# Four layers in one kernel: the ranking's place at the start, the clip's place in the adapter stage, and three smaller moves

## The reference

```python
# layers 1 and 3
q, k, v = x @ Wq, x @ Wk, x @ Wv
attn = softmax(q k^T * 512**-0.5)                       # within a batch, 64 x 64
attn_out = (attn @ v) @ Wp + bp
cms_out = gelu(attn_out @ cW1 + cb1) @ cW2 + cb2 + one_hot(target_codes, 512)
modifier = gelu(concat([attn_out, cms_out]) @ mW1 + mb1) @ mW2 + mb2
x = clip(x + cms_out + modifier, 0.0, 1.0)
# layers 2 and 4
h = gelu(x @ W_down[role] + b_down[role])               # 512 -> 256
y = x + h @ W_up[role] + b_up[role]                     # 256 -> 512
x = (y - mean(y)) * rsqrt(var(y) + 1e-5) * gamma[role] + beta[role]
```

## Time and profile before

| | |
|---|---|
| timed runs | 2047.40, 2045.91, 2047.27 us; median 2047.27 |
| the profiled execution | 2048.77 us, span 2046.9 us, mean granted clock 0.997 |
| TensorE | 2026.1 us busy (99%), 9500 matmuls |
| VectorE | 1513.8 us busy (74%), 2353 instructions |
| ScalarE | 1019.4 us busy (50%) |
| GpSimd | 360.6 us busy (18%) |
| DMA | 169.77 MB, mean 83 GB/s |
| chain that ended last | TensorE 94%, VectorE 4%, ScalarE 1%, issue 1% |

### The profile page before, as it was taken

How to read it: one execution, slowest core, us unless ns; L and a number is a source line. 1 busy time by engine, 2 the same in 40 slices (tenths; PEclk the granted TensorE clock), 3 DMA queues, 4 the chain that set the end, 5 groups by cost and what they waited for, 6 DMA issues and landing times.

```text
span 2046.9 us, 27676 instructions
## 1 busy us (share of the span) xinstructions
PE 2026.1 (99%) x9500; PEld 1692.3 (83%) x9500; DVE 1513.8 (74%) x2353; ACT 1019.4 (50%) x1844; POOL 360.6 (18%) x382
## 2 busy tenths in 40 slices
PE   8999999999999999999999999999999999999998
PEld 7888888888888888888888888888888888888887
DVE  6576677887757667888877666888886766778877
ACT  5464544555355454555436454555544544445552
POOL 0011103222101102233000111233200111032221
PEclk9999999999999999999999999999999999999999
DMA  7401111213321112112460111112243011211142
GB/s 283 172 22 52 52 67 62 72 43 129 145 83 31 63 52 73 38 71 73 145 242 21 52 62 67 37 73 73 72 183 107 11 62 43 77 62 52 57 145 94
DMA packets 42376, 169.77 MB, mean 83 GB/s; under 512 B 5624, under 2 KB 9720, under 8 KB 34808
## 3 DMA queue, kind: packets, MB, share of 16 engines
q1 hardware_dynamic: 42096, 167.97, 23.6%
q10 hardware_dynamic: 144, 0.03, 0.0%
HBM read 146.97 MB, written 21.01 MB: 82 GB/s over the span
## 4 chain that ended last, share of the span: by engine, by line
PE 94%; DVE 4%; ACT 1%; issue 1%; DMA 0%; SPq 0%; DVEq 0%; ACTq 0%
PE psum L667 88%; PE psum L961 1%; PE psum L998 1%; PE psum L742 1%; PE psum L764 1%; DVE acc L1694 0%; ACT xz L1375 0%; DVE fpart L1425 0%; DVE yt L1897 0%; DVE yt L1901 0%; DVE stats L1880 0%; DMA fraw<-fuse_in 0%; PE psum L765 0%; PE psum L744 0%; SPq L421 0%
## 5 line engine op out<-in xcount | busy, mean ns | idle before, releaser
L667 PE MATMUL psum<-hs,wd 128*128 128x512 f32 x1920 | 448.8, 389 | 0.5
L667 PEld LDWEIGHTS psum<-hs,wd 128*128 128x128 f32 x1920 | 360.0, 188 | 76.9 <-DVE acc L1694 2.2
L667 PE MATMUL psum<-cop,wsm 128*128 128x512 f32 x1416 | 354.7, 389 | 0.0
L667 PE MATMUL psum<-aop,wsm 128*128 128x512 f32 x1320 | 333.0, 389 | 0.0
L667 PEld LDWEIGHTS psum<-cop,wsm 128*128 128x128 f32 x1416 | 265.8, 188 | 55.2
L667 PE MATMUL psum<-aop,wsc 128*128 128x512 f32 x1320 | 311.3, 389 | 0.0
L667 PEld LDWEIGHTS psum<-aop,wsm 128*128 128x128 f32 x1320 | 247.7, 188 | 51.5
L667 PEld LDWEIGHTS psum<-aop,wsc 128*128 128x128 f32 x1320 | 247.4, 188 | 51.4
L1670 DVE TENSOR_TENSOR acc<-psum,acc 128x1024 f32<-128x1024 f32 x144 | 175.7, 1220 | 87.4 <-PE psum L667 87.3
L1694 DVE TENSOR_TENSOR acc<-psum,acc 128x512 f32<-128x512 f32 x256 | 167.6, 685 | 84.4 <-PE psum L667 84.3
L1425 DVE TENSOR_TENSOR hs<-hs_raw,hs 128x512 fp32r<-128x512 f32 x256 | 178.8, 706 | 43.8 <-ACT hs_raw L1238 43.8
(11 more groups left out here) (192 smaller groups left out, 3026.3 us busy)
## 6 DMA issues: line engine op xcount, KB each, us to landing
w1m<-m_in SPq DMA_DIRECT2D x32, 1024.0 KB, 4.9
w1c<-c_in SPq DMA_DIRECT2D x32, 512.0 KB, 3.5
w<-c_in SPq DMA_DIRECT2D x32, 512.0 KB, 3.5
w<-m_in SPq DMA_DIRECT2D x32, 512.0 KB, 3.5
gains<-roles_in SPq DMA_DIRECT2D x30, 512.0 KB, 4.7
fw<-fused SPq DMA_DIRECT2D x6, 2048.0 KB, 10.8
fused<-fw SPq DMA_DIRECT2D x4, 2048.0 KB, 7.9
xmid<-x SPq DMA_DIRECT2D x4, 2048.0 KB, 6.7
```

Of the source, the lines that this page charges most:

```text
L667: mm = nc.tensor.matmul(out, lhs(a), rhs(b), start=(start and n == 0), stop=(stop and n == total - 1), skip_group_check=reopened)
```

## The change

Five edits:

1. The ranking is cut in three. Six steps, now `count_lower`, are called inside `operands(0)` behind the second chunk; the other 21, still `place_batches`, stand between `operands(0)` and `operands(1)`.
2. In the adapter's loop the clip is one tile ahead: `clip(i + 4)` behind `normalise(i - 1)` in place of `clip(i + 3)` ahead of `split_x(i + 3)`; the fourth tile's clip moves in front of the loop.
3. The additions of outputs 1 and 2 of the second token block go ahead of the third tile's `split_x`, that of output 3 behind it; all three stood behind `split_h(0)`.
4. The epsilon goes from VectorE (`tensor_scalar` on `veps`) to GpSimd (`tensor_tensor` with a column that holds it).
5. That column, `epsc`, is set once at the start, beside `mhalf`.

```diff
-        mhalf = at("mhalf", [P, 1], F32, CT + 2.53125)
+        power = at("power", [P, 2], F32, CT + 2.53125)
+        mhalf, epsc = power[:, 0:1], power[:, 1:2]
...
+            nc.gpsimd.memset(epsc, EPS).then_inc(made, 1)
+            pool.wait_ge(made, 13)
             pool.wait_ge(brow_loaded, 16)
...
                     for i in range(TILES):
                         e, s = 8 * p + i, i % 2
+                        pool.wait_ge(st_done, 2 * e + 2)
+                        nc.gpsimd.tensor_tensor(veps[:, s, :], mv[:, s, 1:2], epsc, ALU.add).then_inc(ve_done, 1)
                         pool.wait_ge(ve_done, e + 1)
-                        nc.gpsimd.tensor_tensor(rstd[:, s, :], veps[:, s, :], mhalf[:, :], ALU.pow).then_inc(rstd_done, 1)
+                        nc.gpsimd.tensor_tensor(rstd[:, s, :], veps[:, s, :], mhalf, ALU.pow).then_inc(rstd_done, 1)
...
                             minus(u[:, LO, cols], fuse_raw[n][o][:, cols], u[:, HI, cols]).then_inc(fuse_lo, 1)
+                        if (n, k) == (0, 1):
+                            count_lower()
...
-            def place_batches():
+            def count_lower():
...
                 step(nc.vector.tensor_reduce(lower, less_last, AX_X, ALU.add))
+
+            def place_batches():
                 dve.wait_ge(ranked, done)
                 step(nc.vector.tensor_tensor(base, below, lower, ALU.subtract))
...
             compare_batches()
             operands(0)
+            place_batches()
             operands(1)
-            place_batches()
...
                         nc.vector.bn_aggr(mv[:, s, :], stats[:, s, :]).then_inc(st_done, 1)
-                        dve.wait_ge(st_done, 2 * e + 2)
-                        nc.vector.tensor_scalar(veps[:, s, :], mv[:, s, 1:2], EPS, None, ALU.add).then_inc(ve_done, 1)
...
                     clip(2)
+                    add(p, layer, last, 1, 1, 2)
                     split_x(2)
+                    add(p, layer, last, 1, 3)
                     up_part(p, 2)
                     split_h(0)
-                    add(p, layer, last, 1, 1, 2, 3)
+                    clip(3)
                     for i in range(TILES):
                         if i == TILES - 2:
                             split_h(i + 1)
                         if i >= 1:
                             row_stats(i - 1)
                         if i + 3 < TILES:
-                            if i + 3 == TPB:
-                                dve.wait_ge(acc_done, acc_at(p + 1, 0))
-                            clip(i + 3)
                             split_x(i + 3)
                         if i >= 1:
                             normalise(i - 1)
+                        if i + 4 < TILES:
+                            if i + 4 == TPB:
+                                dve.wait_ge(acc_done, acc_at(p + 1, 0))
+                            clip(i + 4)
```

More of the change, by code:

```diff
@@ L577, in _ @@
                            allow_small_or_imprecise_dtypes=True).then_inc(made, 1)
-            nc.gpsimd.memset(mhalf[:, :], -0.5).then_inc(made, 1)
+            nc.gpsimd.memset(mhalf, -0.5).then_inc(made, 1)
             pool.wait_ge(made, 1)
```

## The result

The changed kernel takes 2037.35 us (median of 5, 2036.96 to 2038.39) against 2047.27 (median of 5, 2045.91 to 2048.55): a ratio of 0.9951, 95% interval 0.9939 to 0.9963. It is 9.9 us faster; 14.5 were forecast. The profiled executions differ by more: 2037.42 against 2048.77, spans 2035.5 against 2046.9, 11.4 us.

A forecast was written before the change was run, and what follows sets the result against it. TensorE was taken as the bound, busy 2026.1 of 2046.9 us. Start 5.7 plus passes 1.6, 3.4, 1.5 and 2.5 made 14.7, less 0.2 for rstd: 14.5 off 2047.27, so 2032.8 us; range 2029.5 to 2038.

The forecast's parts named there:

- the clock: Start, third pair of weights onward: without TensorE's long wait the granted clock stays full, gaining 2.7 us.
- the rest of the stage: Adapter tiles after the first stall: TensorE becomes the bound everywhere, gaining 0.6, 2.3, 0.5 and 1.6 us in the four passes.
- the bounds worked out from unknown costs: Whole kernel: clock 2.4 to 2.9, GpSimd addition 0.1 to 0.7, start overrun 0 to 0.5, giving 2032 to 2036 us.
- Ranking in the gaps: Start: ranking fills VectorE's waits, so TensorE's 3.10 us wait before the third pair falls to about 0.1; gain 3.0.
- The first stall: Adapter's fourth tile: its front starts 1.0 us earlier in each of four passes, with a new 0.3 us stall for hz.
- The epsilon: Adapter tiles: VectorE saves 0.15 us each, GpSimd's addition costs 0.2 (bound 0.7); 0.2 us off the sum for rstd.
- Rival B: GpSimd's addition costs 0.7 us and VectorE waits for rstd at pass ends; gain 12.0, 2035.3 us; chance 0.12.
- A: Start gives only the wait: ranking overruns its gaps or the clock falls anyway; gain 11.8, 2035.5 us; chance 0.10.
- C: Adapter pass ends are set by VectorE's chain to the next xs, not TensorE; gain 11, 2036.3 us; chance 0.06.
- D: Adapter: the early clip waits for a later tile's residual transposes; 12 us slower, 2059 us; chance 0.02.

The follow-up runs named there:

- start_only: The kernel before with only the ranking moved into VectorE's gaps: 2042.86 us, ratio 0.998 to the kernel before.
- fw_early: The changed kernel with the second 2 MB of fused weights loaded as soon as their place is free: 2033.83 us, ratio 0.9937 to the kernel before.
- adapter_only: The changed kernel with the 27 ranking steps back behind the second pair: 2041.77 us, ratio 0.9973 to the kernel before.
- eps_vector: The changed kernel with the epsilon's addition back on VectorE instead of GpSimd: 2037.33 us.

## Why the prediction was right, and where its size was off

The direction and the range held, and the gains came by the mechanisms that were forecast; the size was 4.6 us too large, and two terms of the sum make it up: the clock's 2.7 and the rest of the stage in the first three passes. That 2037.35 lies in the range is in part luck: the bounds worked out from unknown costs, 2032 to 2036, miss it, and the upper end of 2038 came from adding up rivals that did not come as described. None of them was the wait for gains.

- *Ranking in the gaps, 3.0.* Right. An overrun of 0.1 was forecast; the gap was 0.22 from full, and TensorE went from the second pair to the third without a break.
- *The clock, 2.7.* The mechanism was right, the size wrong. I read 24.78 against 22.36 us in one execution and took it off the median of executions most of which had paid less, though I had noted that the profiled one lay 1.5 above that median. The other two traces with this wait lost 1.3 and 1.1. start_only's 4.7 leaves 1.6 above the wait of 3.1, which fits them, but its interval reaches from 2.3 to 5.9 in all: how the median shares out between wait and clock stays open that far.
- *The first stall, 1.0 a pass.* Right: the fourth front comes 1.0 to 1.1 us earlier within its pass, with the new stall of 0.24 where 0.3 was forecast. The new stall is too short to appear among the waits.
- *The rest of the stage, 0.6 + 2.3 + 0.5 + 1.6.* The sentence that failed is "so TensorE becomes the bound everywhere". VectorE's own work does fit (periods of 3.80 to 4.26 wherever gains are there), and the fourth pass gave its 1.6. In the first three the transfer of the gains is the next limit. The sum has no term for it. I had written that those loads "queue behind the same loads as before", of the start; the same was true of the adapter stage, and it was the danger: a transfer that starts when a buffer comes free starts earlier with a faster engine, but behind a queue that moves less. fw_early puts a number on it, 3.4 us.
- *The epsilon.* Both prices were seen: 0.54 us beside xz's low part, near my upper bound, and 0.19 in the tail, my value. In the loop rstd is ready just as VectorE ends the first half (520.16 and 520.12) and costs it 0.1 us, which TensorE's pace hides; in the tail a tile takes 2.64 instead of 2.58. The Trainium skill (GPSIMD Engine Reference, section "Key points") says that GpSimd contends with VectorE instructions that have two SBUF inputs; the trace agrees, with 0.54 us beside such a subtraction and 0.19 away from it. Rival B, which I had built on it, still didn't come: B put its price on the last tiles of a pass, and there, as the prediction itself says, no low part stands beside the addition.
- *The rivals.* A, the start without the clock's part, is half true: the clock gave less than forecast, not nothing. C forecast a short adapter stage because VectorE's chain to the next xs would set its end; that chain moved with TensorE, with 4.7 us from the last transpose to the next xs product in the second pass both before (1041.80 to 1046.50) and after (1033.84 to 1038.52). D did not come: no clip waits for a residual.
- *A slip in the sum.* The fourth pass was worked out as 2.6 and went into the sum as 2.5.

The missing 4.6 us: 3.4 for the gains (fw_early), and the rest, 1.2, by subtraction the clock; start_only, 1.0 short of the forecast 5.7, agrees with that. fw_early's 13.4 us are what the change gives without its debt.

## What to carry to other kernels

When an engine is sped up, list the transfers that start when it frees a buffer, and what stands ahead of them in their queue: their slack shrinks by as much as the queue ahead does not move with it. Here the time from the issue of the fused weights to the need for the third tile's gains fell from 16.1 to 12.6 us in the first pass. Put a big transfer ahead by its own earliest condition rather than behind small ones that are wanted every few microseconds. And before a term is priced from one profiled execution, ask whether that execution is typical, by its time and its clock among the timed ones, and read the same stretch in a second trace: here the same wait cost 2.4, 1.3 and 1.1 us of clock in three traces, and the forecast was made from the dearest.

## What the runs showed of the hardware

- Behind a wait of 3.1 us (2.9 in adapter_only) TensorE's granted clock fell in each of the three traces that have it, and the price differed: 2.4, 1.3 and 1.1 us over the same 96 matmuls. Behind 5.4 us it was 2.5 in the one trace, and all eleven executions show the same mean clock, 0.998. Fallen means the lower of the two levels (1.2 and not 2.4 GHz): 0.50 from 32 to 38 us in the kernel before. The Trainium skill (TensorE: Matmul & The Clock Gate, section "Part 1: The HAM clock gate") says of the rise at a kernel's start that it comes at another matmul in another run of the same kernel. These traces show the like for the length of a fall.
- A GpSimd instruction on 128x1 elements is held up by 0.35 us beside a VectorE subtraction with both inputs in SBUF. First the changed kernel, beside xz's low part and in the tail; then eps_vector, where the power alone stands beside it:

```profile
518.97 0.54 POOL L655 TENSOR_TENSOR veps<-mv,power 128x1 f32<-128x1 f32 x1 [35.93 <-DVE mv L1892]
...
536.66 0.19 POOL L655 TENSOR_TENSOR veps<-mv,power 128x1 f32<-128x1 f32 x1 [2.16 <-DVE mv L1892]
```
```profile
2015.27 0.93 POOL L655 TENSOR_TENSOR rstd<-veps,power 128x1 f32<-128x1 f32 x1 [2.88 <-DVE veps L1892]
2019.07 0.55 POOL L655 TENSOR_TENSOR rstd<-veps,power 128x1 f32<-128x1 f32 x1 [2.87 <-DVE veps L1892]
```

The addition ends when the subtraction ends: 518.97 + 0.54 = 519.51, against 518.81 + 0.66 = 519.47 for VectorE's. The power, three times as long by itself, grows by about the same amount, 0.38 against 0.35. That looks like a delay and not like a slower rate; no run varied the subtraction's length to prove it.
